# Softmax of a small attention: row maxima subtracted on VectorE, one exponential per batch on ScalarE

## The chip, the cores and the metric

The kernel runs on one core of a Trainium2 chip. The metric is the device time of one execution in microseconds (us); a kernel's time is the median of its runs. TensorE multiplies matrices, VectorE, ScalarE and GpSimd work elementwise, and each engine takes its instructions strictly in the order of its own queue. They wait for each other by semaphores.

## The reference

Three layers follow each other on an input of 8 batches x 128 rows x 512: a cross attention with 2048 context rows per batch, a latent attention with three branches, and a feed-forward block with experts. The feed-forward block begins with a small self-attention, and that alone is what the change touches:

```python
attn = jnp.einsum('bhqd,bhkd->bhqk', q, k) / np.sqrt(DH)
attn = jax.nn.softmax(attn, axis=-1)
sa = jnp.einsum('bhqk,bhkd->bhqd', attn, v)
sa = sa.transpose(0, 2, 1, 3).reshape(Bb, Tt, C) @ Wo
x = _rmsnorm(src + sa, norm1_w)
```

There are 8 batches, 16 heads and 128 keys for 128 queries, so one batch has 16 score matrices of 128x128: a tile of 128 partitions x 2048 columns in fp32.

## The kernel before

The program is a row of stages with a barrier between them; the one that matters here is `stage_ffn_attend`. Its first part projects queries, keys and values. Then comes a software pipeline over `STEPS`, 0 to 11, written out by hand for each engine: at step k, batch k gets its scores, batch k-1 its row sums, batch k-2 its products with the values, batch k-3 its output projection (`y`).

At step k the engines do the following, each in the order told.

- **TensorE** turns (transposes) half of the weights of batch k-2 (`turn_weights`, line 1717, after GpSimd's `scaled`), computes the 16 score matrices of batch k into PSUM banks 0 to 3 (line 1737), turns the other half, multiplies by the values (line 1757) and does the output projection of batch k-3 (line 1686).
- **VectorE** takes the maxima of all 16 heads of batch k in one reduction (line 1641) and multiplies them by -1/sqrt(32) (line 1643). Then it sums the weights of batch k-1 (line 1647) and takes the reciprocals (line 1649), splits off the low part of the attention output of batch k-2 (line 1652), and adds the projection of batch k-3 to its rows with their moments (lines 1656 and 88 to 90).
- **ScalarE** copies the turned weights of batch k-2 out of PSUM (line 1591), takes the exponentials of batch k (line 1599), copies the values in steps 0 and 1 (line 1603), and takes the high part of the attention output of batch k-2 (line 1609).
- **GpSimd** adds the halves and quarters of the weights of batch k (lines 1566 and 1568), waits for VectorE's reciprocal and scales the weights by it (line 1571).

The exponentials are one ScalarE instruction per head, since each head has its own bias:

```python
for h in range(H):
    a.activation(S[k % 3][:, h], ps[:, h * P:(h + 1) * P], ACT.Exp, scale=HF ** -0.5,
                 bias=mx[:, k % 2, h:h + 1]).then_inc(s_expd, 1)
```

They read the scores from PSUM and write to one of three buffers of the list `S`; the second of them (`RAW`, in the trace `wq_raw`) holds the weights of the output projection before, the third (`CT`, `g_ct`) the compressed keys and values. So ScalarE waits once each, at steps 1 and from 3 on, until the buffer is free. TensorE's scores of the next batch wait until all 16 exponentials have read PSUM.

Of the kernel before, what the change touches and what calls it, by code (L numbers as in the profile page):

```python
# [25 lines left out]
ALU = mybir.AluOpType  # L26
ACT = mybir.ActivationFunctionType
AX = mybir.AxisListType

P = 128  # L30
B = 8
# [4 lines left out]
H = 16  # L36
# [1417 lines left out]
HF = D // H  # L1454
# [16 lines left out]
def stage_ffn_attend(nc, wts, tables, ROWS, XT_hi, XT_lo, LG, prefetch, WC, RAW, W4):  # L1471
# [3 lines left out]
    with ExitStack() as ctx:  # L1475
# [34 lines left out]
        bank = lambda n, w=512: ps[:, n * 512:n * 512 + w]  # L1510
        names = """const_in wkv_in wo_in wq_hi_done wq_lo_done swapped k_swapped vchain
            c_done ct_copied two_done multiplied roped v_done v_copied
            s_done maxed s_expd p_turned pt_copied pv_done scaled ot_hi ot_lo y_done y_read xf_done f_turned xt_hi xt_lo
            logits_done lt_copied logits_turned logits_read wg_hi_done wg_lo_done halved summed rec_done prefetched""".split()
        sems = {n: ctx.enter_context(nc.semaphore("g_" + n)) for n in names}
        (const_in, wkv_in, wo_in, wq_hi_done, wq_lo_done, swapped, k_swapped, vchain,
         c_done, ct_copied, two_done, multiplied, roped, v_done, v_copied,
         s_done, maxed, s_expd, p_turned, pt_copied, pv_done, scaled, ot_hi, ot_lo, y_done, y_read, xf_done, f_turned, xt_hi,
         xt_lo, logits_done, lt_copied, logits_turned, logits_read, wg_hi_done, wg_lo_done, halved, summed, rec_done, prefetched) = (sems[n] for n in names)
        block = ctx.enter_context(nc.Block())  # L1520
        UNITS = [(w, c, t) for w in ("q", "k") for c in range(KC) for t in range(2)]
# [27 lines left out]
        @block.gpsimd  # L1549
        def _(g):  # L1550
            g.wait_ge(wkv_in, 32)
            for n in range(2):
                g.tensor_copy(WK[:, 1, n::2], WK[:, 0, 1 - n::2]).then_inc(k_swapped, 1)
            for u, (w, c, t) in enumerate(UNITS):
                g.wait_ge(multiplied, 2 * (u + 1))
                dst = (QT if w == "q" else KT_)[:, c, t * HALF:(t + 1) * HALF]
                g.tensor_tensor(dst, R[:, u % 2, 0], R[:, u % 2, 1], ALU.add).then_inc(roped, 1)
            g.wait_ge(wq_hi_done, 2)
            g.tensor_tensor(flat(WQ_lo[:]), flat(RAW[:]), flat(WQ_hi[:]).bitcast(F32), ALU.subtract).then_inc(wq_lo_done, 1)
            for b in range(B):  # L1560

                w_ = S[b % 3]
                g.wait_ge(s_expd, H * (b + 1))
                if b:
                    g.wait_ge(summed, b)
                g.tensor_tensor(SS[:], w_[:, :, 0:P // 2], w_[:, :, P // 2:], ALU.add).then_inc(halved, 1)
                g.wait_ge(halved, 2 * b + 1)
                g.tensor_tensor(SS[:, :, 0:P // 4], SS[:, :, 0:P // 4], SS[:, :, P // 4:], ALU.add).then_inc(halved, 1)

                g.wait_ge(rec_done, b + 1)  # L1570
                g.tensor_tensor(w_, w_, sm[:, b % 2].unsqueeze(2).broadcast_to([P, H, P]), ALU.mult).then_inc(scaled, 1)

        @block.scalar
        def _(a):
            a.copy(flat(WQ_hi[:]), flat(RAW[:])).then_inc(wq_hi_done, 1)
            for n in range(4):
                a.wait_ge(c_done, n + 1)
                a.copy(CT[:, n // 2, n % 2 * HALF:(n % 2 + 1) * HALF], bank(n)).then_inc(ct_copied, 1)
            a.wait_ge(const_in, 16 * NC)
            a.copy(flat(WG_hi[:]), flat(WG[:])).then_inc(wg_hi_done, 1)  # L1580
            a.wait_ge(wo_in, 16)
            a.wait_ge(two_done, NU)
            a.copy(flat(WQ_hi[:]), flat(RAW[:])).then_inc(wq_hi_done, 1)
            for k in STEPS:
                if at(k - 2):
                    b = k - 2
                    for n in range(4):
                        a.wait_ge(p_turned, 4 * b + n + 1)
                        if b:
                            a.wait_ge(pv_done, b)  # L1590
                        a.copy(flat(PT[:, 4 * n:4 * n + 4]), bank(5 - n % 2)).then_inc(pt_copied, 1)
                if at(k):
                    a.wait_ge(maxed, 2 * k + 2)
                    if k == 1:
                        a.wait_ge(wq_lo_done, 2)
                    if k >= 3:
                        a.wait_ge(p_turned, 4 * (k - 2))
                    for h in range(H):
                        a.activation(S[k % 3][:, h], ps[:, h * P:(h + 1) * P], ACT.Exp, scale=HF ** -0.5,
                                     bias=mx[:, k % 2, h:h + 1]).then_inc(s_expd, 1)  # L1600
                for b in VALUES.get(k, ()):
                    a.wait_ge(v_done, b + 1)
                    a.copy(V[:, b], bank(4 + b % 4)).then_inc(v_copied, 1)
                if at(k - 2):
                    b = k - 2
                    a.wait_ge(pv_done, b + 1)
                    if b:
                        a.wait_ge(y_done, b)
                    a.copy(OT_hi[:], bank(6)).then_inc(ot_hi, 1)
                for b in TURNS.get(k, ()):  # L1610
                    a.wait_ge(f_turned, b + 1)
                    a.copy(XT_hi[:, :, b * P:(b + 1) * P], bank(b % 4).rearrange("p (k f) -> p k f", k=KC)).then_inc(xt_hi, 1)
            for t in range(2):
                a.wait_ge(logits_done, t + 1)
                a.copy(LT[:, t * HALF:(t + 1) * HALF], bank(t)[0:NL]).then_inc(lt_copied, 1)

        @block.vector
        def _(v):
# [19 lines left out]
            for k in STEPS:  # L1638
                if at(k):
                    v.wait_ge(s_done, k + 1)  # L1640
                    v.tensor_reduce(mx[:, k % 2], ps[:, 0:4 * 512].rearrange("p (h f) -> p h f", f=P), AX.X, ALU.max).then_inc(maxed, 1)
                    v.wait_ge(maxed, 2 * k + 1)
                    v.tensor_scalar(mx[:, k % 2], mx[:, k % 2], -HF ** -0.5, None, ALU.mult).then_inc(maxed, 1)
                if at(k - 1):
                    b = k - 1
                    v.wait_ge(halved, 2 * (b + 1))
                    v.tensor_reduce(sm[:, b % 2], SS[:, :, 0:P // 4], AX.X, ALU.add).then_inc(summed, 1)
                    v.wait_ge(summed, b + 1)
                    v.reciprocal(sm[:, b % 2], sm[:, b % 2]).then_inc(rec_done, 1)
                if at(k - 2):  # L1650
                    v.wait_ge(ot_hi, k - 1)
                    v.tensor_tensor(OT_lo[:], bank(6), OT_hi[:].bitcast(F32), ALU.subtract).then_inc(ot_lo, 1)
                if at(k - 3):
                    b = k - 3
                    v.wait_ge(y_done, b + 1)
                    v.tensor_tensor(ROWS[:, b], bank(7), ROWS[:, b], ALU.add).then_inc(y_read, 1)
                    v.wait_ge(y_read, b + 1)
                    moments(v, c, mom[:, b], ROWS[:, b], stats[:], rs[:, 3, 0:1])
                for b in TURNS.get(k, ()):
                    s_ = slice(b * P, (b + 1) * P)  # L1660
                    v.wait_ge(xt_hi, b + 1)
                    v.tensor_tensor(XT_lo[:, :, s_], bank(b % 4).rearrange("p (k f) -> p k f", k=KC), XT_hi[:, :, s_].bitcast(F32),
                                    ALU.subtract).then_inc(xt_lo, 1)
                if k in NORMS:
                    bs = NORMS[k]
                    s_, w = slice(bs.start, bs.stop), len(bs)
                    link(v.tensor_tensor(rs[:, 0, 0:w], mom[:, s_, 0], mom[:, s_, 0], ALU.mult))
                    link(v.tensor_tensor(rs[:, 0, 0:w], rs[:, 0, 0:w], mom[:, s_, 1], ALU.add))
                    link(v.tensor_scalar(rs[:, 0, 0:w], rs[:, 0, 0:w], RMS_EPS, None, ALU.add))
                    rsqrt_cols(v, c, rs[:, 1, 0:w], rs[:, 0, 0:w], rs[:, 2, 0:w])  # L1670
                    for n, b in enumerate(bs):
                        v.scalar_tensor_tensor(out=ROWS[:, b], in0=ROWS[:, b], scalar=rs[:, 1, n:n + 1], in1=N1[:], op0=ALU.mult, op1=ALU.mult
                                               ).then_inc(xf_done, 1)
# [6 lines left out]
        def _(t_):  # L1680
# [46 lines left out]
            for k in STEPS:  # L1727
# [2 lines left out]
                    turn_weights(k - 2, 1)  # L1730
                if at(k):
                    if k:
                        t_.wait_ge(s_expd, H * k)
                    for h in range(H):

                        q_ = slice(h % 4 * HF, (h % 4 + 1) * HF)
# [32 lines left out]
                for b in TURNS.get(k, ()):  # L1769
                    t_.wait_ge(xf_done, b + 1)  # L1770
                    if b == 0:
                        t_.wait_ge(s_expd, H * B)
                    if b >= 4:
                        t_.wait_ge(xt_lo, b - 3)
                    turn(bank(b % 4), ROWS[:, b]).then_inc(f_turned, 1)
# [573 lines left out]
```

## Time and profile before

| what | us |
|---|---|
| median of 3 runs (lowest, highest) | 3379.67 (3374.82, 3381.36) |
| the profiled execution's own time | 3376.0 |
| its span, first to last instruction | 3374.0 |
| TensorE busy over the span | 3153.1 (93%) |
| VectorE, ScalarE, GpSimd busy | 2480.6, 1718.4, 1746.4 |
| the pipeline of `stage_ffn_attend`, scores of batch 0 to the logits | 2778 to 2903 of the span |

In the profile a row gives start and duration on the span's own clock, engine, line, operation, tiles and shapes, and in square brackets how long the engine had been idle before it and what ended that wait. PE is TensorE, PEld its weight loads, DVE is VectorE, ACT is ScalarE, POOL is GpSimd. [...]

### The profile page before, as it was taken

Reading aid. Unit: us, or ns where it says so; the run is one execution under the profiler, and the core shown is the slowest. Engines: PE = TensorE matmul, PEld = TensorE weight load, DVE = VectorE, ACT = ScalarE, POOL = GpSimd, SP = SyncE. Lnnn points to the kernel's source line nnn. Section 1 sums busy time; section 2 is a strip of 40 time slices with the busy share of each in tenths; the row PEclk is TensorE's granted clock in tenths of the full one; section 3 lists DMA queues with packets and bytes.
Section 4 is the critical chain, followed back from the end, with each engine's and each line's share of the span. In section 5 each row is a group of like instructions: output and inputs, shape, how many; then the busy total and the mean of one; then the engine's idle time right before and its main releaser. Section 6 shows DMA issues by size and latency. Waiting matters only on the chain. (4 is left out here: it accounts for less than half of the span.)

```text
span 3374.0 us, 50847 instructions
## 1 busy us (share of the span) xinstructions
PE 3153.1 (93%) x18116; PEld 2675.1 (79%) x18116; DVE 2480.6 (74%) x3435; ACT 1718.4 (51%) x3267; POOL 1746.4 (52%) x1124
## 2 busy tenths in 40 slices
PE   5999999999999999999999997988989797899996
PEld 4888888888888888888888886867767565678996
DVE  4699999999999999999999996676675734522213
ACT  3466666666666666666666662253453306211000
POOL 4365665566656566556655654051351336246663
PEclk9999999999999999999999997989999899899998
DMA  5544544444454454445445443100000210123220
GB/s 195 155 122 107 126 106 112 122 123 111 106 127 121 108 122 110 113 122 122 109 108 129 106 110 114 43 28 28 1 16 1 70 50 1 59 73 122 85 88 32
DMA packets 216083, 312.50 MB, mean 93 GB/s; under 512 B 28576, under 2 KB 122016, under 8 KB 207648
## 3 DMA queue, kind: packets, MB, share of 16 engines
q1 hardware_dynamic: 213024, 300.84, 34.2%
q0 software_dynamic: 2816, 8.46, 0.7%
q8 instruction: 148, 2.42, 0.3%
q14 instruction: 95, 0.78, 0.1%
HBM read 151.85 MB, written 23.13 MB: 52 GB/s over the span
## 5 line engine op out<-in xcount | busy, mean ns | idle before, releaser
L480 POOL TENSOR_TENSOR es<-es,e 128x512 f32<-128x512 f32 x480 | 621.9, 1296 | 741.4 <-ACT e L556 741.4
L645 DVE TENSOR_TENSOR e_hl<-e,e_hl 128x512 fp32r<-128x512 f32 x512 | 679.7, 1328 | 0.3 <-ACT e L556 0.3
L489 POOL TENSOR_TENSOR c_lo<-raw,c_hi 128x512 fp32r<-128x512 f32 x248 | 426.9, 1721 | 0.0
L636 DVE TENSOR_SCALAR sc<-ps_s,top 128x512 f32<-128x512 f32 x512 | 384.6, 751 | 55.7 <-ACT e L556 1.4
L715 PEld LDWEIGHTS ps_s<-q_hl,k_hl 128*128 128x128 f32 x2048 | 308.5, 190 | 67.6 <-issue 28.4
L632 DVE TENSOR_TENSOR ps_s<-ps_s,right 128x512 f32<-128x512 f32 x512 | 353.4, 690 | 8.8 <-ACT right L565 7.7
L715 PE MATMUL ps_s<-q_hl,k_hl 128*128 128x256 f32 x2048 | 330.8, 284 | 15.4 <-DVE sc L636 15.4
L665 PE MATMUL ps_p<-c_hi,wa 128*128 128x512 f32 x1024 | 339.1, 392 | 4.5 <-PEq L115 4.5
L665 PE MATMUL ps_p<-wa,c_hi 128*128 128x512 f32 x1024 | 337.8, 391 | 0.0
L676 PE MATMUL ps_o<-e_hl,v_hl 128*128 128x256 f32 x2048 | 331.1, 284 | 3.3 <-DVE e_hl L645 3.3
L552 ACT ACTIVATE e_hl<-sc 128x512 fp32r<-128x512 f32 x512 | 324.6, 634 | 1.4 <-PE ps_o L676 1.0
L565 ACT COPY right<-ps_s 128x512 f32<-128x512 f32 x512 | 303.2, 592 | 29.8 <-PE ps_s L715 28.1
L519 ACT CAST v_hl<-ps_p 128x512 fp32r<-128x512 f32 x256 | 150.1, 586 | 329.7 <-PE ps_p L665 329.3
L556 ACT ACTIVATE e<-sc 128x512 f32<-128x512 f32 x512 | 315.9, 617 | 0.0
L519 ACT CAST ot<-ps_p 128x512 fp32r<-128x512 f32 x256 | 150.3, 587 | 276.7 <-PE ps_p L665 270.9
L676 PEld LDWEIGHTS ps_o<-e_hl,v_hl 128*128 128x128 f32 x2048 | 284.3, 193 | 3.8 <-DVE e_hl L645 3.8
L1061 POOL TENSOR_TENSOR s<-s,a_mx 128x1536 f32<-128x1536 f32 x32 | 88.1, 2754 | 308.9 <-DVE a_mx L1212 308.9
L665 PEld LDWEIGHTS ps_p<-c_hi,wa 128*128 128x128 f32 x1024 | 194.0, 189 | 43.1 <-issue 4.9
L665 PEld LDWEIGHTS ps_p<-wa,c_hi 128*128 128x128 f32 x1024 | 192.8, 188 | 37.7
L597 DVE TENSOR_TENSOR ot<-ps_p,ot 128x512 fp32r<-128x512 f32 x256 | 175.8, 687 | 59.2 <-ACT ot L519 58.7
L597 DVE TENSOR_TENSOR v_hl<-ps_p,v_hl 128x512 fp32r<-128x512 f32 x256 | 175.7, 686 | 47.7 <-ACT v_hl L519 47.3
L665 PE MATMUL ps_p<-c_lo,wa 128*128 128x512 f32 x512 | 201.7, 394 | 0.0
(393 smaller groups left out, 7395.5 us busy)
## 6 DMA issues: line engine op xcount, KB each, us to landing
k_hl<-ot SPq DMA_DIRECT2D x1024, 128.0 KB, 2.8
raw<-in_ctx_t SPq DMA_DIRECT2D x64, 1024.0 KB, 6.3
raw<-in_L_ffn_W_experts SPq DMA_DIRECT2D x64, 256.0 KB, 2.9
q_hl<-q_hi_scratch SPq DMA_DIRECT2D x32, 256.0 KB, 5.5
q_hl<-q_lo_scratch SPq DMA_DIRECT2D x32, 256.0 KB, 6.4
raw<-in_L_xattn_Wkv SPq DMA_DIRECT2D x8, 512.0 KB, 4.8
q_hi_scratch<-qa_qh SPq DMA_DIRECT2D x16, 256.0 KB, 2.5
q_lo_scratch<-qa_ql SPq DMA_DIRECT2D x16, 256.0 KB, 3.5
```

Of the source, the lines that this page charges most:

```text
L480: g.tensor_tensor(ES[:, GL], ES[:, GL], e, ALU.add).then_inc(summed, 1)
L489: g.tensor_tensor(C_lo[:, n % 2, k, :], RAW[:, n % 2, k, :], C_hi[:, n % 2, k, :].bitcast(F32), ALU.subtract).then_inc(clo_done, 1)
L552: a.activation(E2[:, s % 2, :, 0, :], sc, ACT.Exp, scale=DH ** -0.5).then_inc(exp_hi, 1)
L556: a.activation(E[:, s % 2], SC[:, s % 2], ACT.Exp, scale=DH ** -0.5).then_inc(expd, 1)
L565: a.copy(RIGHT[:], halves[:, :, 1, :]).then_inc(right_out, 1)
L597: v.tensor_tensor(kv_slice(False, kind, n), ps_view(u, kind), kv_slice(True, kind, n).bitcast(F32), ALU.subtract).then_inc(p_free, 1)
L632: v.tensor_tensor(halves[:, :, 0, :], halves[:, :, 0, :], RIGHT[:], ALU.add).then_inc(halves_added, 1)
L636: v.tensor_scalar(SC[:, s % 2].rearrange("p (j q) -> p j q", j=GRP), halves[:, :, 0, :], top[:, i * (M // P) + kt16:i * (M // P) + kt16 + ...
L645: v.tensor_tensor(E2[:, s % 2, :, 1, :], E[:, s % 2].rearrange("p (j q) -> p j q", j=GRP), E2[:, s % 2, :, 0, :].bitcast(F32), ALU.subtrac ...
L665: mm = t.matmul(ps_p[:, par % 2, :], lhs, rhs, start=m == 0, stop=m == 3 * KC - 1)
L676: mm = t.matmul(ps_o[:, 2 * GL + j // 2, (j % 2) * 256:(j % 2 + 1) * 256], V2[:, kt, GRP * GL + j, :], E2[:, s % 2, j].rearrange("p e q -> ...
L715: mm = t.matmul(ps_s[:, j // 2, (j % 2) * 256:(j % 2 + 1) * 256], K2[:, 2 * GL + j // 2, j % 2, kt * P:(kt + 1) * P], Q2[:, hf, GRP * GL + ...
```

## The change

VectorE no longer multiplies the maxima. It subtracts them from the scores of all 16 heads in one operation, from PSUM into the buffer in SBUF, and ScalarE takes the exponential of that whole buffer in place, with the factor 1/sqrt(32) as its scale and no bias. The three waits for a free buffer go with the write from ScalarE to VectorE (for the third buffer, `CT`, one that the order of ScalarE's queue gave before is now spelled out). TensorE's next scores wait for the subtraction (`shifted`), GpSimd for the one exponential.

```diff
@@ GpSimd
-                g.wait_ge(s_expd, H * (b + 1))
+                g.wait_ge(s_expd, b + 1)
@@ ScalarE
-                    a.wait_ge(maxed, 2 * k + 2)
-                    if k == 1:
-                        a.wait_ge(wq_lo_done, 2)
-                    if k >= 3:
-                        a.wait_ge(p_turned, 4 * (k - 2))
-                    for h in range(H):
-                        a.activation(S[k % 3][:, h], ps[:, h * P:(h + 1) * P], ACT.Exp, scale=HF ** -0.5,
-                                     bias=mx[:, k % 2, h:h + 1]).then_inc(s_expd, 1)
+                    a.wait_ge(shifted, k + 1)
+                    a.activation(S[k % 3], S[k % 3], ACT.Exp, scale=HF ** -0.5).then_inc(s_expd, 1)
@@ VectorE
-                    v.tensor_reduce(mx[:, k % 2], ps[:, 0:4 * 512].rearrange("p (h f) -> p h f", f=P), AX.X, ALU.max).then_inc(maxed, 1)
-                    v.wait_ge(maxed, 2 * k + 1)
-                    v.tensor_scalar(mx[:, k % 2], mx[:, k % 2], -HF ** -0.5, None, ALU.mult).then_inc(maxed, 1)
+                    scores = ps[:, 0:4 * 512].rearrange("p (h f) -> p h f", f=P)
+                    v.tensor_reduce(mx[:, k % 2], scores, AX.X, ALU.max).then_inc(maxed, 1)
+                    if k == 1:
+                        v.wait_ge(wq_lo_done, 2)
+                    if k == 2:
+                        v.wait_ge(v_done, B)
+                    if k >= 3:
+                        v.wait_ge(p_turned, 4 * (k - 2))
+                    v.wait_ge(maxed, k + 1)
+                    v.tensor_tensor(S[k % 3], scores, mx[:, k % 2].unsqueeze(2).broadcast_to([P, H, P]), ALU.subtract).then_inc(shifted, 1)
@@ TensorE
-                        t_.wait_ge(s_expd, H * k)
+                        t_.wait_ge(shifted, k)
...
-                        t_.wait_ge(s_expd, H * B)
+                        t_.wait_ge(shifted, B)
```

VectorE's queue at step 6, before (`g_ps` is PSUM, `g_mx` the maxima, `g_sm` the sums, `wc_raw` the added quarters):

```order
L1641 TENSOR_REDUCE g_mx<-g_ps 128x16
L1643 TENSOR_SCALAR g_mx<-g_mx 128x16
L1647 TENSOR_REDUCE g_sm<-wc_raw 128x16
L1649 RECIPROCAL g_sm<-g_sm 128x16
L1652 TENSOR_TENSOR g_ot_lo<-g_ps,g_ot_hi 128x512
L1656 TENSOR_TENSOR rows<-g_ps,rows 128x512
```

The same place with the change:

```order
L1636 TENSOR_REDUCE g_mx<-g_ps 128x16
L1644 TENSOR_TENSOR g_s<-g_ps,g_mx 128x2048
L1648 TENSOR_REDUCE g_sm<-wc_raw 128x16
L1650 RECIPROCAL g_sm<-g_sm 128x16
L1653 TENSOR_TENSOR g_ot_lo<-g_ps,g_ot_hi 128x512
L1657 TENSOR_TENSOR rows<-g_ps,rows 128x512
```

The subtraction over 2048 columns (`g_s` is the first buffer of `S`) stands where the multiplication over 16 stood: behind the maxima of batch k and ahead of the sums of batch k-1.

ScalarE's queue at two steps of the pipeline, before:

```order
L1591 COPY g_pt<-g_ps 128x512 x4
L1599 ACTIVATE g_ct<-g_ps,g_mx 128x128 x16
L1609 CAST g_ot_hi<-g_ps 128x512
L1591 COPY g_pt<-g_ps 128x512 x4
L1599 ACTIVATE g_s<-g_ps,g_mx 128x128 x16
L1609 CAST g_ot_hi<-g_ps 128x512
```

The same place with the change:

```order
L1591 COPY g_pt<-g_ps 128x512 x4
L1594 ACTIVATE g_ct<-g_ct 128x2048
L1603 CAST g_ot_hi<-g_ps 128x512
L1591 COPY g_pt<-g_ps 128x512 x4
L1594 ACTIVATE g_s<-g_s 128x2048
L1603 CAST g_ot_hi<-g_ps 128x512
```

The order of the rest is as it was; sixteen instructions that read PSUM and the maxima are one that reads and writes the buffer.

## Rows read from the trace of the kernel before

**Rows 1.** Busy time by engine in the steady part, three steps of the pipeline.
```profile
core 0: us, PE busy (x) PEld busy (x) DVE busy (x) ACT busy (x) POOL busy (x), PEclk, DMA share, GB/s
2824.55:2853.41 28.86, 21.92 (x277) 17.07 (x276) 16.60 (x27) 20.61 (x64) 21.62 (x9) 1.00 0.00 1
```

**Rows 2.** GpSimd in order of time, the scalings of batches 0 to 4 and 6.
```profile
2792.17 3.61 POOL L1571 TENSOR_TENSOR g_s<-g_s,g_sm 128x2048 f32<-128x2048 f32 x1 [1.09 <-DVE g_sm L1649]
...
2803.76 3.61 POOL L1571 TENSOR_TENSOR wq_raw<-wq_raw,g_sm 128x2048 f32<-128x2048 f32 x1 [4.32 <-DVE g_sm L1649]
...
2814.93 3.61 POOL L1571 TENSOR_TENSOR g_ct<-g_ct,g_sm 128x2048 f32<-128x2048 f32 x1 [3.91 <-DVE g_sm L1649]
...
2824.55 3.61 POOL L1571 TENSOR_TENSOR g_s<-g_s,g_sm 128x2048 f32<-128x2048 f32 x1 [2.33 <-DVE g_sm L1649]
...
2834.17 3.61 POOL L1571 TENSOR_TENSOR wq_raw<-wq_raw,g_sm 128x2048 f32<-128x2048 f32 x1 [2.33 <-DVE g_sm L1649]
...
2853.41 3.61 POOL L1571 TENSOR_TENSOR g_s<-g_s,g_sm 128x2048 f32<-128x2048 f32 x1 [2.34 <-DVE g_sm L1649]
```

**Rows 3.** TensorE in order of time, step 5.
```profile
2828.22 1.10 PE L1717 MATMUL g_ps<-g_ident,g_s 128*128 128x128 f32 x8 [1.59 <-POOL g_s L1571]
2829.24 1.17 PE L1737 MATMUL g_ps<-g_kt,g_qt 32*128 32x128 f32 x32
```

**Rows 4.** VectorE in order of time, step 5 and the start of step 6.
```profile
2830.72 2.29 DVE L1641 TENSOR_REDUCE g_mx<-g_ps 128x16 f32<-128x2048 f32 x1
2833.05 0.17 DVE L1643 TENSOR_SCALAR g_mx<-g_mx 128x16 f32<-128x16 f32 x1
2833.13 0.68 DVE L1647 TENSOR_REDUCE g_sm<-wc_raw 128x16 f32<-128x512 f32 x1
...
2838.01 0.69 DVE L1652 TENSOR_TENSOR g_ot_lo<-g_ps,g_ot_hi 128x512 fp32r<-128x512 f32 x1 [3.91 <-ACT g_ot_hi L1609]
...
2840.34 2.29 DVE L1641 TENSOR_REDUCE g_mx<-g_ps 128x16 f32<-128x2048 f32 x1
```

**Rows 5.** ScalarE in order of time, step 5.
```profile
2833.25 4.24 ACT L1599 ACTIVATE g_ct<-g_ps,g_mx 128x128 f32<-128x128 f32 x16 [1.14 <-DVE g_mx L1643]
2837.27 0.70 ACT L1609 CAST g_ot_hi<-g_ps 128x512 fp32r<-128x512 f32 x1
```

**Rows 6.** Groups by line and shape: busy us, mean ns, idle before.
```profile
L1208 DVE TENSOR_TENSOR s<-a_ps,a_causal 128x1536 f32<-128x1536 f32 x32 | 56.2, 1756 | 39.6 <-PE a_ps L1308 39.5
...
L1626 DVE CAST wa<-wa 128x1024 fp32r<-128x1024 f32 x4 | 3.0, 805 | 0.0
...
L1115 ACT ACTIVATE s<-s 128x1536 f32<-128x1536 f32 x32 | 47.6, 1487 | 61.6 <-POOL s L1061 61.6
...
L1583 ACT CAST wa<-wq_raw 128x2048 fp32r<-128x2048 f32 x1 | 1.9, 1899 | 56.6 <-PE g_ps L1711 56.6
```

**Rows 7.** TensorE in order of time, steps 1 to 3.
```profile
2787.37 1.17 PE L1737 MATMUL g_ps<-g_kt,g_qt 32*128 32x128 f32 x32 [2.58 <-ACT g_s L1599]
...
2797.47 1.07 PE L1717 MATMUL g_ps<-g_ident,g_s 128*128 128x128 f32 x8 [3.61 <-ACT g_v L1603]
2798.48 1.77 PE L1737 MATMUL g_ps<-g_kt,g_qt 32*128 32x128 f32 x32
...
2807.42 1.97 PE L1717 MATMUL g_ps<-g_ident,wq_raw 128*128 128x128 f32 x8 [3.51 <-POOL wq_raw L1571]
2809.32 2.09 PE L1737 MATMUL g_ps<-g_kt,g_qt 32*128 32x128 f32 x32
```

**Rows 8.** VectorE in order of time, the maxima of batch 0.
```profile
2780.54 2.29 DVE L1641 TENSOR_REDUCE g_mx<-g_ps 128x16 f32<-128x2048 f32 x1 [3.55 <-PE g_ps L1737]
```

**Rows 9.** TensorE's busy time and granted clock around step 3.
```profile
core 0: us, PE busy (x), PEclk, DMA share, GB/s
2805.00:2813.00 8.00, 5.58 (x48) 0.57 0.01 2
```

**Rows 10.** Lines 645 and 632: duration in ns (least, median, most).
```profile
L645 DVE TENSOR_TENSOR e_hl<-e,e_hl x512: 681/1392/1772, 119.4 to 2040.3; 128x512 fp32r<-128x512 f32 x171
...
L632 DVE TENSOR_TENSOR ps_s<-ps_s,right x512: 678/690/700, 114.8 to 2036.2; 128x512 f32<-128x512 f32 x171
```

**Rows 11.** Line 1641: what ended VectorE's idle time before it (us, times).
```profile
  PE g_ps L1737: 20.5, 4
```

More of the change, by code:

```diff
@@ L1512, in stage_ffn_attend @@
             c_done ct_copied two_done multiplied roped v_done v_copied
-            s_done maxed s_expd p_turned pt_copied pv_done scaled ot_hi ot_lo y_done y_read xf_done f_turned xt_hi xt_lo
+            s_done maxed shifted s_expd p_turned pt_copied pv_done scaled ot_hi ot_lo y_done y_read xf_done f_turned xt_hi xt_lo
             logits_done lt_copied logits_turned logits_read wg_hi_done wg_lo_done halved summed rec_done prefetched""".split()
@@ L1517, in stage_ffn_attend @@
          c_done, ct_copied, two_done, multiplied, roped, v_done, v_copied,
-         s_done, maxed, s_expd, p_turned, pt_copied, pv_done, scaled, ot_hi, ot_lo, y_done, y_read, xf_done, f_turned, xt_hi,
+         s_done, maxed, shifted, s_expd, p_turned, pt_copied, pv_done, scaled, ot_hi, ot_lo, y_done, y_read, xf_done, f_turned, xt_hi,
          xt_lo, logits_done, lt_copied, logits_turned, logits_read, wg_hi_done, wg_lo_done, halved, summed, rec_done, prefetched) = (sems[n] for n in names)
```

## The prediction

> **What bounds the kernel now.** Read the busy times by stretch first. The change touches one stage of about 125 us, and in its steady part [rows 1] no engine is busy throughout: TensorE 21.92, GpSimd 21.62, ScalarE 20.61 and VectorE 16.60 of 28.86 us, with almost no DMA. So the stage is not held by the load of an engine but by a ring of waits that the batches go round. No other engine works on a later stage meanwhile; the stretch after it starts when the last batch is through, so what a step of the ring gains or loses the program gains or loses.
>
> Next, GpSimd in order of time [rows 2]: the scaling of the weights (line 1571) starts at 2814.93, 2824.55, 2834.17 and, two batches on, at 2853.41. That is 9.62 us per batch, and each time GpSimd sat 2.33 us waiting for VectorE's reciprocal. TensorE [rows 3] waited 1.59 us for that scaling, turned the weights of batch 3 (2828.22), and computed the scores of batch 5 (2829.24, ended 2830.41). VectorE [rows 4] took their maximum from 2830.72 to 2833.01, scaled it, and only then, from 2833.13, summed batch 4, whose reciprocal releases the scaling at 2834.17. That is **ring one**: scaling, turning, scores, maximum, sum, reciprocal, scaling of the next batch. From the scaling's start at 2824.55 to the scores' arrival at about 2830.47 is 5.92, from the maximum's start to the next scaling 3.45: 9.37 us.
>
> **Ring two** runs through ScalarE [rows 5]: maximum (2830.72), sixteen exponentials (2833.25), the attention output's high part (2837.27), then VectorE again (2838.01, after waiting 3.91 for it), three more VectorE operations, and the next maximum at 2840.34: 9.62 us. Ring two sets the pace, but ring one has only 9.62 - 9.37 = 0.25 us to spare.
>
> **The change part by part.**
> *Exponentials.* Sixteen of 128x128, 4.24 us in all [rows 5], become one of 128x2048 from SBUF. The nearest rows [rows 6] are one exponential of 128x1536 from SBUF, 1.487 us, and a ScalarE pass over 128x2048, 1.90. I take 1.90; the bounds are 1.49 and 1.98 (1.487 x 2048/1536). ScalarE gets 8 x 2.34 = 18.7 us of busy time back.
> *Subtraction.* VectorE loses a 0.17 us multiplication and gets one operation of 128x2048 that reads PSUM. An operation of the same kind over 1536 columns of PSUM takes 1.756 [rows 6], and the maximum over these very 2048 columns 2.29 [rows 4]. I take 2.29; bounds 1.44 and 4.6, under the rivals. Added at this place: 2.29 - 0.17 = **2.12 us per batch**.
> *Ring two* loses 2.2 (the output's high part started 4.02 after the exponentials' start, 1.82 after the new one's) and gains 2.12: about 9.54.
> *Ring one* has the subtraction and no exponential. The sum of batch k-1 stands behind the subtraction of batch k in VectorE's queue, GpSimd's scaling waits for that sum, the turning for the scaling, the next scores stand behind the turning. 9.37 + 2.12 = **11.49 us**. Ring one takes over, and each step is 11.49 - 9.62 = 1.87 longer. What becomes late is the reciprocal; GpSimd's wait of 2.33 grows to about 4.2, and VectorE now waits for scores too.
> *Waits that move.* Scores of the next batch wait for the subtraction instead of all exponentials: in the steady part they stand behind the turning anyway, so nothing. The waits moved from ScalarE to VectorE (the weight split's read of the buffer, the value products, the turning of batch k-3) are for things that are over: the split ends at about 2782.8, eight us before batch 1's subtraction would start. Queued behind them would be the sums. No DMA moves.
> *Head.* Scores of batch 1 waited for the exponentials until 2787.37 [rows 7]. Now the subtraction of batch 0 ends at 2780.54 [rows 8] + 2.32 + 2.29 = 2785.15, so they start 2.2 earlier, which batch 1's subtraction uses up: the first scaling stays at about 2792.1 [rows 2]. Its end, 2795.7, releases the turning of batch 0, which before waited till 2797.47 for ScalarE's copies behind the sixteen exponentials [rows 7]: -1.7. Then maximum to scaling is 2.12 longer: the second scaling comes at **+0.4**. From it to the third was 11.17 [rows 2], already ring one, with TensorE slow: **+2.12**. Third to seventh: four steps of 1.87, **+7.5**. From the seventh scaling (2853.41) on no subtraction is left, and GpSimd's halving, VectorE's sum and the last scaling run as before: 0. Sum with TensorE at full clock: **+10.0 us**.
>
> *TensorE's clock.* TensorE's idle before each turning grows from 1.59 [rows 3] to 1.59 + 1.87 = 3.46 us. Two idle stretches of that length are in the trace [rows 7]. [...] Against 1.10 and 1.17 in the steady part [rows 3] with starts 1.02 apart, that is 0.60 and (1.90 - 1.02) + (2.09 - 1.17) = 1.80 us in ring one. Per step the bounds are 0 and 1.80. A step that ran slow leaves the next one less idle, so I take half, 0.9: 4 x 0.9 = **+3.6**. Taken for the copies and output products: nothing, they lie beside ring one.
> [...]
>
> Sum: 10.0 + 3.6 = **+13.6 us**. Against the profiled execution's own 3376.0 that is 3389.6. The median of the three runs, 3379.67, lies 3.7 above it, inside their spread of 6.5; on the median I predict **3393.3**.
>
> **The rivals.**
> (a) *Cold at every step.* Ring one with 1.80 each time: 10.0 + 7.2 = +17.2, 3396.9. For: the idle of 3.46 is as long as the two in rows 7. Against: one of those cost a third of it. Chance 0.15.
> (b) *A dear subtraction.* VectorE operations slow down when both inputs lie in SBUF and GpSimd is at work: line 645 has a median of 1392 ns for 512 columns and 681 at best, where line 632, with an input in PSUM, keeps to 678 to 700 [rows 10]. Twice the price, 4.6, would add 2.3 for each of the eight batches (the head's two included), 18.4 on top of 13.6: 3411.7. Against: the subtraction reads PSUM and sixteen maxima. Chance 0.07.
> (c) *A cheap subtraction.* A VectorE conversion of 1024 columns takes 0.805 [rows 6]; twice that, less the 0.17 that an operation of 16 columns takes [rows 4], is 1.44. That is 0.85 less for each of eight batches, and TensorE's idle grows by 1.02 alone, too little to slow it: 10.0 - 6.8 = +3.2, 3382.9. But that pass has one input, this one two. Chance 0.05.
> (d) *Ring two keeps the pace*, the side that is not slower. Then a step is 9.54, 0.08 shorter, five times, and the head gives its 1.7: -2.1, 3377.6. It decides at the slack between the scores' arrival and the maximum's start: at 2.1 us or more ring one stays hidden. The trace shows 0.25, and in four of eight batches the maximum waited for the scores, 20.5 us in all [rows 11]. Chance 0.08.
> (e) *ScalarE's saving comes through.* If ScalarE held each step and the subtraction cost nothing there, 18.7 us less: 3361. Against: the subtraction lies in both rings. Chance 0.03.
> [...]
>
> **How the numbers follow.** The forecast has the remaining 0.62. A measurement of this kernel tells about 0.2%, 6.8 us, from no change. Slower: (a), (b), and the forecast but for 0.02 where its full-clock end of +10.0 meets noise, 0.82. Faster: (e), 0.03. Within: the rest, 0.15. The range goes from +10.0 on the lowest run, 3374.8 (3384.8), to +17.2 on the highest, 3381.4 (3398.6), with a little for a subtraction over 2.29: 3384 to 3401. It leaves out (b), (d) and (e), 0.18.
>
> **What would show it.** Right: the subtraction near 2.29 and the exponential near 1.90; scaling starts 11.5 to 13.3 apart; GpSimd's wait for the reciprocal at 4 us or more; VectorE idle before each maximum, waiting for scores; ScalarE's busy time down by 18 to 19; the granted clock of the steady part under 1.00. Wrong: steps of 9.5 with no VectorE wait for scores (d); a subtraction over 4 us (b) or under 1.6 (c); steps of exactly 11.5 at full clock would leave the size too high by 3.6.

## The result and the profile after

| | median us (lowest to highest, runs) | ratio to before, 95% interval |
|---|---|---|
| before | 3378.66 (3374.82 to 3381.36, 5) | |
| changed kernel | 3396.17 (3389.49 to 3401.69, 5) | 1.0048 [1.0035, 1.0061] |

The change makes the kernel 0.48% slower, 17.5 us. (Two runs of the kernel before have joined the three that stand ahead of the prediction.) The profiled execution of the changed kernel took 3397.29 us with a span of 3395.2, which is 21.2 more than before. Of that, 4.06 us arose ahead of the stage, in code that is the same: the first scores began at 2782.44 after 2778.38. From the first scores to the addition of the logits, **the pipeline** from here on, took 141.46 us where it had taken 124.13. That is +17.33, about the difference between the medians. The runs below are therefore compared by this length as well as by their medians.

GpSimd in order of time, one whole step and the scalings beside it (start, duration, then the wait before it and what ended it):

```profile
2835.36 3.61 POOL L1571 TENSOR_TENSOR g_s<-g_s,g_sm 128x2048 f32<-128x2048 f32 x1 [5.58 <-DVE g_sm L1650]
2838.93 2.36 POOL L1566 TENSOR_TENSOR wc_raw<-wq_raw 128x1024 f32<-128x1024 f32 x1
2841.37 1.27 POOL L1568 TENSOR_TENSOR wc_raw<-wc_raw 128x512 f32<-128x512 f32 x1
2847.52 3.61 POOL L1571 TENSOR_TENSOR wq_raw<-wq_raw,g_sm 128x2048 f32<-128x2048 f32 x1 [4.89 <-DVE g_sm L1650]
...
2860.96 3.61 POOL L1571 TENSOR_TENSOR g_ct<-g_ct,g_sm 128x2048 f32<-128x2048 f32 x1 [6.18 <-DVE g_sm L1650]
```

The scalings start 12.16 and 13.44 us apart where they were 9.62 apart [rows 2], and GpSimd's wait for the reciprocal grew from 2.33 to about 5 or 6. The whole rows of distances between scaling starts, from batches 0 and 1 to batches 6 and 7, are:

| kernel | steps (us) | pipeline |
|---|---|---|
| before | 11.59, 11.17, 9.62, 9.62, 9.62, 9.62, 8.45 | 124.13 |
| changed | 13.03, 13.33, 12.85, 12.16, 13.44, 13.12, 8.43 | 141.46 |

VectorE in order of time, within the same step:

```profile
2841.88 2.29 DVE L1636 TENSOR_REDUCE g_mx<-g_ps 128x16 f32<-128x2048 f32 x1 [2.73 <-PE g_ps L1738]
2844.27 2.29 DVE L1644 TENSOR_TENSOR g_ct<-g_ps,g_mx 128x2048 f32<-128x2048 f32 x1
2846.48 0.68 DVE L1648 TENSOR_REDUCE g_sm<-wc_raw 128x16 f32<-128x512 f32 x1
2847.19 0.25 DVE L1650 RECIPROCAL g_sm<-g_sm 128x16 f32<-128x16 f32 x1
2849.13 0.69 DVE L1653 TENSOR_TENSOR g_ot_lo<-g_ps,g_ot_hi 128x512 fp32r<-128x512 f32 x1 [1.69 <-ACT g_ot_hi L1603]
```

This answers to [rows 4]. The quarters were ready at 2842.64 (2841.37 + 1.27, GpSimd's rows), yet their sum began at 2846.48, behind the subtraction. And VectorE, which had gone from its last operation of a step straight to the next maximum, now sits idle for 2.73 us until the scores come. What ended VectorE's idle time before the maxima (us, times) answers to [rows 11], 20.5 us in four batches:

```profile
  PE g_ps L1738: 31.4, 8
```

Now every batch's maximum waits for TensorE. TensorE in order of time, the turning and the scores in the four steps between the third and the seventh scaling:

```profile
2826.18 1.38 PE L1718 MATMUL g_ps<-g_ident,g_ct 128*128 128x128 f32 x8 [3.55 <-POOL g_ct L1571]
2827.48 2.09 PE L1738 MATMUL g_ps<-g_kt,g_qt 32*128 32x128 f32 x32
...
2839.02 1.09 PE L1718 MATMUL g_ps<-g_ident,g_s 128*128 128x128 f32 x8 [3.26 <-POOL g_s L1571]
2840.05 1.71 PE L1738 MATMUL g_ps<-g_kt,g_qt 32*128 32x128 f32 x32
...
2851.18 1.97 PE L1718 MATMUL g_ps<-g_ident,wq_raw 128*128 128x128 f32 x8 [2.76 <-POOL wq_raw L1571]
2853.08 2.09 PE L1738 MATMUL g_ps<-g_kt,g_qt 32*128 32x128 f32 x32
...
2864.62 1.97 PE L1718 MATMUL g_ps<-g_ident,g_ct 128*128 128x128 f32 x8 [2.79 <-POOL g_ct L1571]
2866.52 1.77 PE L1738 MATMUL g_ps<-g_kt,g_qt 32*128 32x128 f32 x32
```

Against [rows 3] the wait for the scaling grew from 1.59 to around 3 us, and the turning and the scores take up to 1.97 and 2.09 instead of 1.10 and 1.17. The busy time by engine over the five steps from batch 1's scaling to batch 6's (the columns of [rows 1]) has the clock beside it:

```profile
2809.18:2874.08 64.90, 45.34 (x460) 35.98 (x460) 36.75 (x41) 23.47 (x31) 35.92 (x15) 0.82 0.00 1
```

TensorE's granted clock (PEclk, a share of its full clock) is 0.82. The same five steps before (2803.76 to 2853.41) had 0.93, since their first one was slow already (0.57 between 2805 and 2813 [rows 9]), and the steady part had 1.00 [rows 1]. ScalarE, the engine that the change relieves, in the same step (here one exponential stands for the sixteen of [rows 5]):

```profile
2846.60 1.92 ACT L1594 ACTIVATE g_ct<-g_ct 128x2048 f32<-128x2048 f32 x1 [2.31 <-DVE g_ct L1644]
```

It is 2.3 us shorter than sixteen, and ScalarE had waited 2.31 us for its input. The saving lies in idle time.

### The profile page after: what moved, and what is told of

The parts are those of the page before. It is cut to its first block and busy times, and to the rows that moved or that the text cites. A ratio compares the mean times of both kernels' runs of the same rounds, so it can differ in the third digit from the quotient of the medians.

```text
span 3395.2 us, 50728 instructions
## 1 busy us (share of the span) xinstructions
PE 3161.8 (93%) x18116; PEld 2683.6 (79%) x18116; DVE 2497.7 (74%) x3435; ACT 1702.2 (50%) x3147; POOL 1745.6 (51%) x1124
```

## The experiments

The theory was that ring one (scaling, turning, scores, maximum, subtraction, sum, reciprocal) sets the pace, with a slowed TensorE in it. The first four runs are edits of the changed kernel that each cut or spare one link. Their median of the kernel before, taken on the same chip, is 3378.85; that of the next four 3379.43, of the last three 3378.11.

### Scores ahead of the turning

```diff
 for k in STEPS:
-    if at(k - 2):
-        turn_weights(k - 2, 0)
-        turn_weights(k - 2, 1)
     if at(k):
...
         mm.then_inc(s_done, 1)
+    if at(k - 2):
+        turn_weights(k - 2, 0)
+        turn_weights(k - 2, 1)
```

> Order theory: the loss comes from where the subtraction stands, between the scaling of one batch and the reciprocal that releases the next. With the scores ahead of the turning on TensorE, maximum and subtraction run while GpSimd still scales; the ring is then scaling 3.6, halving 2.4, quartering 1.3, sum and reciprocal 1.1, some 8.4 us, and the ring through ScalarE, 9.5, sets the step. Scaling starts 9.5 to 9.7 apart (12.2 to 13.4 in the changed kernel), 17 to 21 us less than the changed kernel, 3374 to 3378, no slower than before. Price theory: the new operations cost the time wherever they stand; the durations are the same, so the time stays near 3396. Clock theory: most of the loss is TensorE's slow clock; then about half comes back, 3386 to 3390, as the idle stretches are shared out anew.

Measured: 3379.39 us, ratio 0.9997 [0.9986, 1.0008], pipeline 123.89. Cutting the link from the scaling to the next scores takes the whole loss away, so the loss went through that link. But the median is 1.4 us above the expected stretch, and the steps aren't even, so that the pipeline of the kernel before comes back as a sum of shorter and longer ones: 8.36, 8.35, 12.42, 9.47, 12.80, 9.47, 8.44. ScalarE and, under it, VectorE in order of time in a long step show a wait that wasn't foreseen:

```profile
2841.00 0.59 ACT L1603 CAST g_ot_hi<-g_ps 128x512 fp32r<-128x512 f32 x1 [3.23 <-PE g_ps L1687]
```

```profile
2841.62 0.69 DVE L1653 TENSOR_TENSOR g_ot_lo<-g_ps,g_ot_hi 128x512 fp32r<-128x512 f32 x1 [4.91 <-ACT g_ot_hi L1603]
```

The output's high part has one buffer. ScalarE had to wait until TensorE's output projection of the batch before (line 1687) had read it, and VectorE, with the next maximum queued behind, waited 4.91 us for ScalarE.

### The sum ahead of the subtraction

```diff
 v.tensor_reduce(mx[:, k % 2], scores, AX.X, ALU.max).then_inc(maxed, 1)
+if at(k - 1):
+    sums(k - 1)
...
 v.tensor_tensor(S[k % 3], scores, mx..., ALU.subtract).then_inc(shifted, 1)
-if at(k - 1):
-    b = k - 1
...
+if at(k - 1) and not at(k):
+    sums(k - 1)
```

`sums` holds the wait for the quarters, the sum and the reciprocal, unchanged.

> Order theory: with sum and reciprocal of the batch before between maximum and subtraction, the subtraction leaves the ring through GpSimd (back to about 9.3 us) and only the ring through ScalarE has it, now with sum and reciprocal in it too: 9.5 + 1.0 = 10.5. Steps of 10.4 to 10.7, pipeline 128 us against 141 in the changed kernel and 124 before; 3381 to 3386. Price theory: the same operations on the same engine, 3396.

Measured: 3380.12 us, ratio 1.0008 [0.9999, 1.0017], pipeline 128.02, steps 13.37, 10.78, 10.09, 10.10, 10.78, 10.10, 8.96. The pipeline is the expected one to 0.02 us, but its steps lie on both sides of the expected 10.4 to 10.7, and the first is as long as with the change. The median lies 0.9 below its stretch, and its interval takes in the +3.9 that the pipeline gives. GpSimd's row in a steady step, where the subtraction no longer stands ahead of the reciprocal:

```profile
2831.44 3.61 POOL L1571 TENSOR_TENSOR wq_raw<-wq_raw,g_sm 128x2048 f32<-128x2048 f32 x1 [2.31 <-DVE g_sm L1636]
```

GpSimd waits 2.31 again, as before the change (2.99 and 3.00 in the steps of 10.78). Moving the sum and its wait within VectorE's queue gives back 13.4 of the 17.3 us. So what costs is not that the subtraction runs, but that the sum stands behind it.

### Sixteen exponentials, from SBUF

```diff
-a.activation(S[k % 3], S[k % 3], ACT.Exp, scale=HF ** -0.5).then_inc(s_expd, 1)
+for h in range(H):
+    i = a.activation(S[k % 3][:, h], S[k % 3][:, h], ACT.Exp, scale=HF ** -0.5)
+i.then_inc(s_expd, 1)
```

> The subtraction stays, the exponential goes back to sixteen instructions per batch, now from SBUF and without a bias. Order theory: ScalarE is not in the ring that sets the pace, so its saving is worth little: the ring through ScalarE becomes 9.5 + 2.3 = 11.8 us, still under the 12.2 to 13.4 of the steps; within 4 us of the changed kernel, 3394 to 3401. Rival (ScalarE's saving counts in full): 8 x 2.3 = 18 us more, 3414.

Measured: 3398.27 us, ratio 1.0058 [1.0044, 1.0071], pipeline 140.84. ScalarE in order of time, its exponentials in one step:

```profile
2843.42 3.30 ACT L1595 ACTIVATE g_ct<-g_ct 128x128 f32<-128x128 f32 x16 [3.16 <-DVE g_ct L1646]
```

Each batch's exponentials take 3.30 instead of 1.91, and the time does not move beyond the noise (1.0048 [1.0035, 1.0061] with one exponential). The half of the change that saves something saves it where nobody waits. That is rival (e), the saving that comes through, excluded by a run.

### Fill for TensorE

```diff
+if 2 <= k <= B:
+    for j in range(18 if k > 2 else 40):
+        t_.transpose(bank(4)[:, j % 4 * P:(j % 4 + 1) * P], I[:], I[:])
 for b in TURNS.get(k, ()):
```

> Eighteen idle-time transposes of the identity (40 in step 2) after TensorE's output projection, into a PSUM bank that is free there; their results are never read. Clock theory as a term of the order theory: the ring stays at 11.5 to 11.6 us, the slow clock's share (about 1.3 us per step in the profile of the changed kernel) goes: granted clock 0.95 or more in the steady part, scaling starts 11.5 to 11.8 apart, 5 to 7 us less than the changed kernel, 3389 to 3391. If the clock were only a symptom: no gain, or a loss where a filler delays the turning, 3396 to 3400.

Measured: 3390.73 us, ratio 1.0035 [1.0022, 1.0049], pipeline 134.54, steps 13.36, 11.58, 11.65, 11.64, 11.64, 11.65, 8.43. GpSimd in a steady step, and under it TensorE's busy time and granted clock over five steps:

```profile
2823.10 3.61 POOL L1571 TENSOR_TENSOR g_s<-g_s,g_sm 128x2048 f32<-128x2048 f32 x1 [4.37 <-DVE g_sm L1650]
...
2834.74 3.61 POOL L1571 TENSOR_TENSOR wq_raw<-wq_raw,g_sm 128x2048 f32<-128x2048 f32 x1 [4.38 <-DVE g_sm L1650]
```

```profile
2799.87:2858.03 58.16, 46.81 (x557) 1.00 0.01 1
```

TensorE in order of time, the first turning and the second with the scores behind them:

```profile
2790.17 1.97 PE L1718 MATMUL g_ps<-g_ident,g_s 128*128 128x128 f32 x8 [4.37 <-POOL g_s L1571]
2792.07 2.09 PE L1738 MATMUL g_ps<-g_kt,g_qt 32*128 32x128 f32 x32
...
2803.54 1.09 PE L1718 MATMUL g_ps<-g_ident,wq_raw 128*128 128x128 f32 x8 [1.21 <-POOL wq_raw L1571]
2804.56 1.17 PE L1738 MATMUL g_ps<-g_kt,g_qt 32*128 32x128 f32 x32
```

Transposes whose result nobody reads, put into TensorE's idle time, bring the granted clock of these five steps from 0.82 to 1.00 and leave ring one at full clock: 11.64 us. The pipeline is 6.9 us shorter than the changed kernel's. By the medians it is 5.4, where the two intervals overlap; that the gain is real is read from the steps. The 6.9 is what a slow TensorE cost this kernel behind the first turning, not what the change added to that cost. Step by step the fill saves 1.75, 1.20, 0.52, 1.80 and 1.47 from the second to the sixth, and 0.5 behind the last scaling; the first step is 0.33 longer, since the fill stands behind its turning. In the second step the kernel before had a slow TensorE too: a granted clock of 0.50 over its turning and scores, 1.97 and 2.09 us [rows 7].

### Scores first in the kernel before

The same edit of TensorE's order as in the first experiment, in the kernel before.

> The same move of the scores ahead of the turning, in the kernel before. Order theory: there the ring through ScalarE (9.62 us) sets the step and the one through GpSimd has 0.25 to spare, so the move is worth little in the steady part, and some 2 to 5 us where a step waited for the scores (the 11.17 us step): pipeline 118 to 122 us against 124, 3374 to 3377. If moving the scores were a good in itself, whatever ring binds: 17 us less, as in the changed kernel, 3362.

Measured: 3377.32 us, ratio 0.9993 [0.9984, 1.0002], pipeline 120.35, steps 8.35, 9.07, 11.13, 9.60, 9.61, 9.60, 8.43. The median is 0.3 us above the expected stretch, and its interval takes in no change at all; the pipeline is within its stretch. GpSimd in order of time, a steady step:

```profile
2827.11 3.61 POOL L1571 TENSOR_TENSOR wq_raw<-wq_raw,g_sm 128x2048 f32<-128x2048 f32 x1 [2.33 <-DVE g_sm L1649]
...
2836.72 3.61 POOL L1571 TENSOR_TENSOR g_ct<-g_ct,g_sm 128x2048 f32<-128x2048 f32 x1 [2.32 <-DVE g_sm L1649]
```

With ring one cut the steady step stays at 9.6. So in the kernel before it was ring two that set the pace, as the prediction had it; only the head, where ring one bound, got shorter (the first three steps take 28.55 us where they took 32.38, though the third alone is longer).

### Ring one without the subtraction

The kernel before, with one maximum for all 16 heads of a row and one exponential with it as bias, straight from PSUM. Of the edit the exponential is shown.

```diff
-for h in range(H):
-    a.activation(S[k % 3][:, h], ps[:, h * P:(h + 1) * P], ACT.Exp, scale=HF ** -0.5,
-                 bias=mx[:, k % 2, h:h + 1]).then_inc(s_expd, 1)
+a.activation(S[k % 3], ps[:, 0:4 * 512].rearrange("p (h f) -> p h f", f=P), ACT.Exp, scale=0.25 * HF ** -0.5,
+             bias=mx[:, k % 2, 0:1]).then_inc(s_expd, 1)
...
```

> One exponential per batch without any subtraction: the kernel before, with one maximum per row over all heads as the bias of a single exponential that reads PSUM. What it leaves out: the heads' own maxima, and the scores are taken at a quarter of their scale, so the weights are others and the experts' loads too; it is to be read by the pipeline's own stretch, from the first scores to the logits. Order theory: with 16 exponentials made one and nothing added to VectorE, the ring through GpSimd stays at 9.4 and sets the step; steps of 9.3 to 9.7 (the change: 12.2 to 13.4), pipeline 116 to 121 us against 124 before and 141 with the change. If the one large exponential itself were what costs, the pipeline stays over 130.

Measured: 3375.91 us, ratio 0.9988 [0.9979, 0.9997], pipeline 120.65, steady steps 9.43 and 9.44. Its weights are others, so the pipeline and the steps are what is compared. ScalarE and GpSimd in a steady step:

```profile
2836.53 1.98 ACT L1598 ACTIVATE g_ct<-g_ps,g_mx 128x2048 f32<-128x2048 f32 x1 [0.95 <-DVE g_mx L1642]
```

```profile
2837.46 3.61 POOL L1571 TENSOR_TENSOR wq_raw<-wq_raw,g_sm 128x2048 f32<-128x2048 f32 x1 [2.15 <-DVE g_sm L1648]
```

Even with nothing added on VectorE, one exponential in place of sixteen buys 0.19 us per steady step: from ring two at 9.62 to ring one at 9.43, which the prediction had read off the trace as 9.37. With the head it is 3.5 us of the pipeline.

### Two output buffers, and the scaling in halves

The first experiment's new wait is mended in the changed kernel, with the scores ahead of the turning, by a second buffer for the attention output (in a tile that is free by then), with the high part ahead of the exponential in ScalarE's queue.

```diff
-OT_hi = sb("ot_hi", [P, D], F32R)
+OT_hi = sb("ot_hi", [P, D], F32R)[:], WS_hi[:, 0]
...
+if at(k - 2):
+    b = k - 2
+    a.wait_ge(pv_done, b + 1)
+    if b >= 2:
+        a.wait_ge(y_done, b - 1)
+    a.copy(OT_hi[b % 2], bank(6)).then_inc(ot_hi, 1)
 if at(k):
...
```

> The changed kernel with the scores first, and two buffers for the attention output's high and low part, whose high part ScalarE takes ahead of the exponential. With the scores first alone the steps were 8.4 to 12.8 us, and the long ones had ScalarE waiting up to 3.2 us for TensorE's output projection to free the buffer. Order theory: that wait is the new ring; without it the steps come to 8.4 to 9.2, pipeline 112 to 116 us, 3367 to 3372, 0.2 to 0.35% under before. Rival: the steps are held by the load of VectorE or by the slow clock; then it stays at 3376 to 3380.

Measured: 3370.0 us, ratio 0.9975 [0.9963, 0.9987], pipeline 116.80, which is 0.8 over the expected stretch; steps 8.95 and 9.30 to 9.35 in turn from the third on, the longer ones over the expected 9.2. The long and short steps of the first experiment are gone. What is left is the turning, which waits for GpSimd's scaling, and the scores behind it. A second edit halves that wait:

```diff
-g.tensor_tensor(w_, w_, sm[:, b % 2].unsqueeze(2).broadcast_to([P, H, P]), ALU.mult).then_inc(scaled, 1)
+for n in range(2):
+    h_ = slice(n * H // 2, (n + 1) * H // 2)
+    g.tensor_tensor(w_[:, h_], w_[:, h_], sm[:, b % 2, h_].unsqueeze(2).broadcast_to([P, H // 2, P]), ALU.mult).then_inc(scaled, 1)
...
-    t_.wait_ge(scaled, b + 1)
+    t_.wait_ge(scaled, 2 * b + 1)
...
+if n == 2:
+    t_.wait_ge(scaled, 2 * b + 2)
```

> As the run with two buffers, and GpSimd scales in two halves of 8 heads, so that TensorE turns the first half while the second is scaled. If GpSimd's scaling is in the ring, 1 to 4 us less than with two buffers alone, 3364 to 3369; if the ring of GpSimd's own three operations (7.3 us and the reciprocal) sets the step, the same within 1.5 us.

Measured: 3365.47 us, ratio 0.9955 [0.9942, 0.9969], pipeline 112.88, steps of 8.49 to 8.60. That is 4.5 us less than with two buffers alone by the medians, 3.9 by the pipeline, where 1 to 4 were expected. GpSimd in order of time:

```profile
2826.68 3.75 POOL L1573 TENSOR_TENSOR wq_raw<-wq_raw,g_sm 128x1024 f32<-128x1024 f32 x2 [1.09 <-DVE g_sm L1652]
2830.39 2.36 POOL L1566 TENSOR_TENSOR wc_raw<-g_ct 128x1024 f32<-128x1024 f32 x1
2832.83 1.29 POOL L1568 TENSOR_TENSOR wc_raw<-wc_raw 128x512 f32<-128x512 f32 x1
2835.28 3.75 POOL L1573 TENSOR_TENSOR g_ct<-g_ct,g_sm 128x1024 f32<-128x1024 f32 x2 [1.16 <-DVE g_sm L1652]
```

GpSimd's own three operations are 7.4 of the 8.6 us, and the rest is the sum and the reciprocal that it must wait for. The ring is now GpSimd's. This version beats both kernels.

### Is the change needed in that version?

The same edits were put on the kernel before, without the change: once all of them, and once with TensorE's old order (half of the turning ahead of the scores). The version with the change ran again beside them.

> The kernel before with every edit of the two-output, halved-scaling version (scores first, two output buffers, the output's high part ahead of the exponentials, scaling in halves), and without the change: multiplication and sixteen exponentials from PSUM stay. Theory: the change is needed in that arrangement, because the next scores wait for all sixteen exponentials, and turning, copies, value products and the output's high part stand behind them and ahead of the next exponentials. Ring: exponentials 4.24, scores 1.2, then from the turning to the end of the high part 4.9, about 10.4 us per step; about 0.8 us longer than before in each of some six steps: median 3381 to 3387. Rival: the change adds nothing there and GpSimd sets the pace all the same: steps of 8.5 to 8.7, median 3364 to 3369.

> As the run above, but TensorE keeps its old order, half of the turning ahead of the scores. Theory: the ring is then exponentials 4.24, scores 1.2, the other half of the turning to the end of the high part 3.6, and waits of 0.1: steps of about 9.1, pipeline 118 to 122, median 3373 to 3378, so a part of the gain comes without the change and the rest, some 0.5 us per step, only with it. Rival: the edits give the whole gain without the change, steps of 8.5 to 8.7 and a median of 3364 to 3369. Second rival: nothing comes, ring two keeps 9.6 and the median 3377 to 3381.

> The changed kernel with scores first, two output buffers and halved scaling once more, on the chip of the two runs above and against the same runs of the kernel before, to set them beside it: steps of 8.5 to 8.6, median 3363 to 3368, ratio 0.995 to 0.997.

Measured:

| kernel | median us, ratio [95%] | steady steps | pipeline |
|---|---|---|---|
| all edits, no change | 3380.5, 1.0005 [0.9996, 1.0015] | 10.24 | 127.08 |
| the same, turning first | 3373.54, 0.9986 [0.9977, 0.9996] | 8.84 | 120.85 |
| all edits and the change | 3364.52, 0.9962 [0.9949, 0.9976] | 8.52 to 8.60 | 111.38 |

TensorE and ScalarE in order of time, the first of the three in a steady step:

```profile
2834.58 1.17 PE L1740 MATMUL g_ps<-g_kt,g_qt 32*128 32x128 f32 x32 [1.89 <-ACT wq_raw L1607]
2835.69 1.10 PE L1721 MATMUL g_ps<-g_ident,g_s 128*128 128x128 f32 x8
```

```profile
2830.30 4.24 ACT L1607 ACTIVATE wq_raw<-g_ps,g_mx 128x128 f32<-128x128 f32 x16
2836.38 1.07 ACT L1593 COPY g_pt<-g_ps 128x512 f32<-128x512 f32 x2 [1.85 <-PE g_ps L1721]
```

Without the change the scores wait 1.89 us for the sixteen exponentials to let go of PSUM, the turning stands behind the scores, and ScalarE waits 1.85 us for the turning: the ring of about 10.4 that was foreseen measures 10.24, its median 0.5 below the expected stretch. With the turning first it is 8.84 (expected 9.1), and part of the gain comes without the change. The version with the change is 9.0 us faster than that one (3373.54 - 3364.52). Of the 9.5 us between their pipelines 5.2 come from the first two steps (11.62 and 10.60 against 8.48 and 8.53), 1.1 from the third, 0.25 to 0.32 from each later one, and 1.9 from behind the last scaling. Most of the 1.9 can't be put down to the change: the version with the change is the kernel of the halved scaling over again, and from its last scaling to the logits that took 39.35 us in the first profile and 37.83 here. Between the first and the last of the three the change is the only difference, and the steady step goes from 10.24 to about 8.55. So the change is worth something once nobody waits for the release that is queued behind its operation: in the halved version's rows above the quarters are ready at 2834.12 and their sum starts at 2834.24, so the subtraction ahead of it holds nothing up. And the next scores wait for the subtraction alone (2.29 us), and get their PSUM back earlier than from sixteen exponentials (4.24).

## Why the prediction was right, and where its sizes were off

The forecast was 3393.3 and slower; 3396.17 is inside its range, 2.9 above. By the medians the change cost 17.5 us, 3.9 more than the +13.6 forecast; 1.0 of that doesn't show in the 2.9, because the median before came out 1.0 lower with five runs than with three. The stage was to give all of the +13.6; it gave 17.33.

- **Durations.** Subtraction 2.29 forecast, 2.29 measured in all eight; exponential 1.90 forecast, 1.91 measured. ScalarE's exponentials went from 33.96 us to 15.31, 18.65 less where 18.7 was forecast. Rivals (b) and (c), a dear and a cheap subtraction, are out. The waits for a free buffer that moved to VectorE held it for a tenth of a microsecond at most: every subtraction started 0.03 to 0.11 us after its maximum had ended.
- **Which ring.** Ring one took over as forecast, (d) is out: the maxima wait for the scores in every batch, and cutting either of two links of ring one removes most or all of the loss. Ring two's 9.54 is seen in the first experiment, where short steps that nothing else holds are 9.47.
- **Ring one at full clock.** 11.49 forecast, 11.64 in the filled kernel at a granted clock of 1.00. The added operation was put at 2.12, its duration less that of the multiplication; from the maximum's start to the next scaling the filled kernel takes 5.65 (2829.09 to 2834.74) where it was 3.45, so it added 2.20. The rest is the maximum's start, some 0.1 us after the scores' end when it has to wait for them.
- **Head.** Batch 0's scaling came at the forecast place (0.08 us earlier, counted from the first scores) and its turning 1.72 earlier (forecast 1.7). But that turning found TensorE slow, and from its start to the scores' end 3.65 us passed, at a granted clock of 0.57, where it had been 2.78 at 0.75 [rows 7]. So the second scaling came at +1.36, not +0.4. The third step was +2.16, forecast +2.12.
- **Clock, the term that was mis-sized.** The prediction took half of 1.80 us for each of four steps, 3.6 in all. The 1.80 is what a turning and its scores had cost more than in the steady part, in the one step before that had a granted clock of 0.50 over both (2807.42 to 2811.41 [rows 7]); the half of it was the author's estimate, and no run shows it. From the turning's start to the scores' end the four steps took 3.39, 2.74, 3.99 and 3.67, at granted clocks of 0.60, 0.77, 0.50 and 0.57, where the steady part before took 2.19 at 1.00 [rows 3]: 1.20, 0.55, 1.80 and 1.48 more, 5.0 in all. The run with fill bears this out: it shortens the same four steps by 1.20, 0.52, 1.80 and 1.47, 4.99 in all. The head adds 0.87 by the rows, forecast at nothing; the fill doesn't reach it. The last part of the stage is 0.7 longer, also forecast at nothing, and the transposes of the normalized rows there took 2.63 instead of 1.91, at a granted clock of 1.00 in both kernels. But two profiles of one kernel differ by 1.5 in that part (39.35 and 37.83 above), so the 0.7 can't be called the change's.

Added up: 5.0 for the clock in the four steps, 0.87 in the head and 0.7 behind are 6.6 and leave 17.3 - 6.6 = 10.7 where +10.0 was forecast for a full clock. The mechanism and its place were right; the clock was put too low, at 3.6 where 5.0 is shown twice and 5.9 with the head by the rows. Rival (a), cold at every step (3396.9), was nearest in time, but by another sum: it had 7.2 in the four steps, and one of them paid a third of the full price. What failed is the inference that took half because "a step that ran slow leaves the next one less idle". The idle time ahead of the four turnings did fall, from 3.55 and 3.26 to 2.76 and 2.79, but the price did not fall with it: the two shorter waits came ahead of the two dearest steps (1.80 and 1.48). The mean of the four steps is 1.26 of 1.80 us, above the half. In the run with fill, from its second turning to that of batch 5, with the waits filled and a granted clock of 1.00, each turning takes 1.09 and the scores behind it 1.17. Why the price varied so from step to step is open.

Two slips in the working moved no term of the sum. Rival (c), at 3382.9, lies below the range from 3384 too, so the range leaves out 0.23 and not 0.18. And in ring two four VectorE operations follow the output's low part, not three (lines 1656 and 88 to 90).

## What to carry to other kernels

Before shortening work on an engine, find the ring that sets the pace and ask in which place of it the replacement stands: an operation of 2.29 us on an engine that was busy for 16.60 of 28.86 us made every steady step 2.0 us longer even at full clock (9.62 to 11.64), because the row sums that another engine waited for were queued behind it, while 18.7 us saved on ScalarE bought nothing that could be measured. Where an engine's queue holds two releases, put the one that somebody waits for first, and look for what shares a single buffer before moving anything. With longer waits TensorE also ran slower here, at a granted clock of 0.82 over five steps against 1.00 with the waits filled: four longer steps cost 5.0 of the 7.2 us that four times the 1.80 would have been, so such a cost belongs in the price of a longer ring, and half was too little.

## What the runs showed of the hardware that was not expected

- The length of one wait did not decide how the next burst ran. After 3.26 us of idle the turning took 1.09 and the scores 1.71, at a granted clock of 0.77; after 2.76 us they took 1.97 and 2.09, at 0.50 (the rows of TensorE above).
- VectorE's subtraction started 0.10 us after the maximum's end where a wait for a free buffer was queued between them (2841.88 + 2.29 = 2844.17 to 2844.27), and 0.03 in batch 0, which has no such wait. That these waits are the cause was not tried apart.
- Sixteen exponentials of 128 columns took 3.30 us from SBUF without a bias, against 4.24 from PSUM with one [rows 5].
- GpSimd's scaling took little longer in smaller pieces: 3.61 us in one operation and 3.75 in two.
- In the profiles of the eleven experiments the first scores of this stage came anywhere from 2772.79 to 2784.77 us, with the same code ahead of them. Two spans taken from one profile each can differ by that without any change, and the part of 4.06 us here belongs to it.
- The pipeline, too, differs between profiles of the same kernel: 112.88 and 111.38 us in the two runs of the version with all edits and the change. The difference lies in the last stretch, from the last transposes of the normalized rows to the turning of the logits: 12.49 us at a granted clock of 0.63 (2878.53 to 2891.02) and 10.94 at 0.73 (2876.72 to 2887.66). A difference of that size between two pipelines says nothing by itself; the steps between scalings agreed to 0.01 us in the two.
